# A graph network on one core: drains on POOL at every fourth block of an edge pass

## The reference

```
h = relu(layernorm(x)); x = x + L0(h)   # typed attention: k[src], q[dst], v[src] per edge, softmax over the edges of dst
h = relu(layernorm(x)); x = x + L1(h)   # gated attention: z[src], segment_max, segment_sum, sigmoid gate
h = relu(layernorm(x)); x = x + L2(h)   # U[dst] += w ** [1, 1, 2, 6] * x.sum(1)[src]; U @ coeff.T
h = relu(layernorm(x)); x = x + L3(h)   # three convolutions:
    m = concat(h[dst], h[src], edge_attr) @ W + b
    h = segment_sum(m, dst)             # with relu after the first two
```

## Time and profile before

| | |
|---|---|
| median of 3 timed runs | 11907.75 us |
| lowest and highest | 11903.76 and 11925.74 us |
| span of the profiled execution | 13242.4 us |
| POOL busy in it | 9106.3 us (69%) |
| DVE busy | 4015.6 us (30%) |
| ACT busy | 3476.7 us (26%) |
| PE busy | 1352.0 us (10%) |
| moved by DMA | 919.05 MB, 69 GB/s on average |

### The profile page before, as it was taken

How to read it: one execution, slowest core, us unless ns; L and a number is a source line. 1 busy time by engine, 2 the same in 40 slices (tenths; PEclk the granted TensorE clock), 3 DMA queues, 4 the chain that set the end, 5 groups by cost and what they waited for, 6 DMA issues and landing times. The chain is left out here.

```text
span 13242.4 us, 37433 instructions
## 1 busy us (share of the span) xinstructions
PE 1352.0 (10%) x6735; PEld 1005.3 (8%) x6735; DVE 4015.6 (30%) x5472; ACT 3476.7 (26%) x4561; POOL 9106.3 (69%) x8728
## 2 busy tenths in 40 slices
PE   5200000020000000395000000200000000000000
PEld 3100000010000000273000000200000000000000
DVE  2255555544445544695111111011111101111110
ACT  2333223312222222375232222122211212221121
POOL 3677777767777776402777777577777767777776
PEclk7655555555555555697555555555555555555555
DMA  7333333313333333001222222111111111111111
GB/s 277 133 97 97 98 95 95 100 34 90 98 95 94 94 99 81 14 1 32 61 58 61 58 58 60 40 50 46 49 46 46 49 39 50 46 49 46 46 49 42
DMA packets 404823, 919.05 MB, mean 69 GB/s; under 512 B 171046, under 2 KB 195277, under 8 KB 389496
## 3 DMA queue, kind: packets, MB, share of 16 engines
q0 software_dynamic: 278944, 386.91, 13.3%
q1 hardware_dynamic: 121832, 529.42, 10.9%
q10 hardware_dynamic: 3824, 0.50, 0.0%
HBM read 456.45 MB, written 459.77 MB: 69 GB/s over the span
## 5 line engine op out<-in xcount | busy, mean ns | idle before, releaser
L864 POOL DMA_INDIRECT arena<-tab,src x6256 | 6549.8, 1047 | 2894.4 <-issue 2101.0
L2244 DVE TENSOR_TENSOR_SCAN arena<-cv_keep,arena 128x768 f32<-128x768 f32 (+1 forms) x476 | 752.0, 1627 | 5757.2 <-issue 4526.3
L864 POOL DMA_INDIRECT arena<-tab,spread x1564 | 1644.1, 1051 | 518.5 <-issue 518.5
L2106 ACT COPY arena<-arena 128x1472 f32<-128x1472 f32 x204 | 545.3, 2673 | 3003.9 <-DMA arena<-tab,src 3003.9
L2111 ACT COPY arena<-arena 128x1472 f32<-128x1472 f32 (+1 forms) x204 | 588.3, 2884 | 551.8 <-DVE arena L2244 431.2
L1089 PE MATMUL e_t<-ident,arena 128*68 128x128 f32 (+1 forms) x2 | 0.8, 397 | 4433.5 <-PEq L1433 2223.3
L2168 PE MATMUL cv_t<-ident,arena 128*81 128x128 f32 (+1 forms) x294 | 137.9, 469 | 2917.7 <-ACT arena L2118 1528.3
L2105 ACT COPY arena<-arena 128x368 f32<-128x368 f32 x68 | 55.3, 813 | 1353.7 <-issue 1325.1
L2182 PE MATMUL cv_t<-ident,arena 128*64 128x128 f32 (+1 forms) x3 | 1.3, 425 | 3391.1 <-ACT arena L2111 3391.1
L951 ACT ACTIVATE ae_prob<-arena 128x92 f32<-128x92 f32 x68 | 17.1, 251 | 1228.8 <-remote 1152.7
L1089 PEld LDWEIGHTS e_t<-ident,arena 128*68 128x68 f32 (+1 forms) x2 | 0.3, 134 | 4433.9 <-issue 4433.9
(11 more groups left out here) (370 smaller groups left out, 6943.0 us busy)
## 6 DMA issues: line engine op xcount, KB each, us to landing
rows<-arena SPq DMA_DIRECT2D x68, 1506.5 KB
arena<-tab,src POOLq DMA_INDIRECT x6256
rows3b<-arena SPq DMA_DIRECT2D x136, 736.0 KB
rows<-arena SPq DMA_DIRECT2D x68, 920.0 KB
rows<-arena SPq DMA_DIRECT2D x68, 828.0 KB
tab<-arena SPq DMA_DIRECT2D x49, 1024.0 KB
q_start<-arena SPq DMA_DIRECT2D x32, 1564.0 KB
arena<-q_start SPq DMA_DIRECT2D x68, 736.0 KB
```

Of the source, the lines that this page charges most:

```text
L864: pool.indirect_dma_start(out=rows[b][:, j, :], out_offset=None, in_=table, in_offset=bass.IndirectOffsetOnAxis(ap=idx[:, at:at + 1].bitca ...
L2106: nc.scalar.copy(chain[:, 0:D, 1:C1], rin[b].rearrange("p j f -> p f j")).then_inc(s_in, 1)
L2244: ins = v.tensor_tensor_scan(out=part, data0=keep[:, 0:(f1 - f0) * C1], data1=part, initial=0.0, op0=ALU.mult, op1=ALU.add)
```

## The change

Inside `gather_columns`, behind the wait at the head of a block and ahead of its gathers, POOL now runs a drain where the block's number is a multiple of SWEEP = 4 and not zero. That is at blocks 4, 8, 12 and so on up to 64: 16 drains in a pass, 80 in the program. A drain holds the engine's sequencer until the engine has finished what it was given before. Nothing else is different: the gathers, their order, the waits and the buffers stay, and no instruction of another engine moves.

```diff
@@ -76,6 +76,7 @@
 BATCH = 3
 UNIT = 8
 ARENA = 25600
+SWEEP = 4
 SEG = 32
 SEGS = -(-J // SEG)
 JP = SEGS * SEG
@@ -859,6 +860,8 @@
     for c in range(NC):
         b = c % 2
         wait(pool, s_rows, c - 1)
+        if c and c % SWEEP == 0:
+            pool.drain()
         for j in range(C):
             at = c * C + j
             pool.indirect_dma_start(out=rows[b][:, j, :], out_offset=None, in_=table,
```

## The result

The change makes the kernel slower: 12546.64 us (12543.96 to 12548.2) against 11905.76 us, a ratio of 1.0537 (95% interval 1.0524 to 1.0550). That is 640.9 us, or 8.01 us for each of the 80 drains. The forecast was 0.45 us each.

A forecast was written before the change was run, and what follows sets the result against it. POOL's gathers were taken to bound every pass. Drain plus restart less the usual gap, 0.45 us for each of 80 drains, gave 36 us on the 11907.75 us median: 11944 us, range 11890 to 12100 us.

The forecast's parts named there:

- What bounds the kernel: In the five gather passes POOL sets the pace, one gather every 1.25 us; time added there moves the end equally.
- Is that buffer there in an execution that isn't profiled? The trace speaks against it.: Behind POOL's gathers: a buffer slowing blocks from 28.8 to 32.2 us was taken as absent from timed runs.
- The drain itself: At each new drain: the drain's own time, nearest rows 0.21 us and 0.04 to 0.05 us.
- The restart: From a drain's end to POOL's next gather: 0.28 to 0.92 us, less the usual 0.30 us gap.
- The transfers in flight: Rival at each new drain: it waits for transfers in flight, 1.8 us extra, 141 us in all, 12049 us; chance 0.12.
- The buffer stays full: Rival in the passes: a real, full buffer binds POOL at 1.40 us a gather; 105 us more, 12013 us; chance 0.09.
- emptied cheaply: Rival in the passes: drains empty a real slow buffer cheaply, 192 us less in all, 11716 us; chance 0.10.
- The whole tail is paid and nothing comes back: Rival at each new drain: the full 9.9 us tail is paid, 792 us in all, 12700 us; chance 0.05.
- slow buffer: Behind POOL in the rivals: something paced at 1.40 us per gather that holds POOL when full.
- The chances: For the whole kernel: slower by over 0.2% 0.62, same 0.28, faster 0.10.
- bare cost of drain and restart: Main case at the 80 new drains: 0.45 us each, 11944 us, own range 11905 to 11975; chance 0.64.

The follow-up runs named there:

- second recording: The kernel before, unchanged, profiled once more: span 11903.9 us, against 13242.4 us when it was first profiled.
- Kernel 8: Kernel before with, at the change's 80 places, a wait until the consumer is through with the block, then a drain: 13226.79 us, ratio 1.1110.
- kernels 13 and 14: Kernel before plus 55 drains, at every sixth block: at its head 12160.02 us (ratio 1.0213), 15 gathers later 12111.87 us (1.0172).

## Why the prediction was wrong

The place was right and the size was not: 36 us were forecast for the sum, and 640.9 us measured. Point by point:

- *What bounds the kernel.* Right. POOL's flow of gathers sets the pace of the passes, and the 639.2 us that it gained in gaps came out of the end in full. The changed kernel's groups of four blocks take the 115 us they took before and the 8 us of a hole, and ACT and DVE have no part in it.
- *"Is that buffer there in an execution that isn't profiled? The trace speaks against it."* This is the step that failed. I saw two things, blocks that got slower and long tails of the drains at the ends of stages, and made one cause of them. Since the blocks' slowness couldn't be in the timed runs, I struck out the tails as well. The second recording has the one without the other: all gaps are 0.3 us, and the drain of L908 takes 22.5 us in it against 25.1 us. The 9.9 us tail of the last stage in rows 8 was nearly all real; without the disturbance it is 8.22 us (the drain ends at 11901.83, the last gather at 11893.61).
- *The drain itself.* Mis-sized: 0.04 to 0.21 us were taken from the drains of L1063 and L198. They were thought quick because POOL had been quiet. Kernel 8 shows that quiet doesn't help. The drains of L1063 and L198 follow no more than two DMAs since the last drain, and 0.21 us for two and 0.05 us for none fit 0.0817 us a DMA. The row to be read was the drain of L1619, behind 197 DMAs, which is shown below; the sum had at most 0.21 us.
- *The restart.* Within its bounds: 0.72 us from the drain's end to the next gather, against 0.28 to 0.92 us.
- *The transfers in flight* (first rival, 12049 us). Its mechanism is there as a floor of some 1.6 us that shows behind short runs; behind 92 gathers it is covered by the clearing. Of the two passages of the Trainium skill weighed beside the sum, Perfetto Trace Analysis ("DMA Instruction — SWDGE (GPSIMD)") says that a gather's row ends when its last descriptor is written; the trace agrees, with ACT starting 1.45 us behind that end. PSUM — Partial Sum Buffer ("Engine vs sequencer instructions") says that a drain waits until its engine is fully idle. From the two the prediction took it that nothing beyond the rows is waited for. The runs show 7.57 us beyond them behind 92 gathers.
- *The buffer stays full, or is emptied cheaply* (12013 and 11716 us). There is no such buffer holding POOL back in a timed run.
- *The whole tail is paid and nothing comes back* (12700 us, chance 0.05). This is what happened in size, with 7.57 us of tail for the 9.9 us of the disturbed recording and 0.42 us of restart beyond the usual gap; but what stands behind the tail is not the slow buffer of the rivals. The argument against it, that the trace has tail and stalls only together, was wrong on the first recording itself. The stage of L1619 runs undisturbed there (its gathers and scatters come with gaps of 0.30 us as in the second recording), and its last DMA is this:

```profile
5489.67 1.05 POOL L1649 DMA_INDIRECT arena<-s_tab,first  x1 [0.30 <-issue]
```

The drain of L1619 begins at 5473.1 us and lasts 25.8 us, so it ends 8.14 us after this DMA. That is a tail without a stall, and the second recording has the same 8.14 us.

- *The chances.* 0.62 for slower was on the right side, though most of it rested on the bare cost of drain and restart, which is not what was paid. The range, up to 12100 us, left out the one case whose price stood in a row of the trace.

Shown by the runs: the 0.0817 us a gather up to 112, that idling of up to 15.8 us doesn't reduce it, that in a pass at one pace a clearing without a drain sets in at 113 to 115 open gathers, and what it takes there (kernels 13 and 14). Only argued: that the 0.0817 us are the sequencer's bookkeeping of each transfer, and that in plain flow it is hidden because the sequencer is some twelve gathers (15 us) ahead. Open: what disturbed the first recording, whether the count or the time sets off a clearing, how far it goes outside the passes, and the longer holes of the first two passes.

No version beats the kernel before. Its own long drains at the ends of stages could not be shortened by met waits.

## What to carry to other kernels

A drain on POOL in the middle of a run of indirect DMAs is priced by the gathers since the last drain, here 0.08 us each up to about 112 and at least some 1.6 us right behind a gather, plus 0.7 us of restart. Idle time ahead of it doesn't lower the 0.08 us each; where only landing matters, a wait on the semaphore is cheaper (2.28 against 8.01 us here). Read a new drain's cost from the existing drain that has most like it in front. And where the profiled span and the timed runs differ by 11%, record again before a term is taken out of the sum on the ground of that difference.

## What the runs showed of the hardware

- A drain of POOL takes 0.0817 us for each indirect DMA that POOL has issued since the last drain (tails of 3.16 us behind 38 and 9.20 us behind 112), after they have landed. Some holes of the first two passes are up to 3.7 us longer. An idle time of 4.2 to 15.8 us ahead of the drain takes nothing off (7.55 to 7.64 us behind 92 or 93 DMAs, all 80 times).
- In a pass, at 113 to 115 open gathers, POOL clears on its own, up to the last head of a block (46 of 138 left with a head at 92, 38 of 138 with one at 100), with no gap in the gathers. At the end of the convolutions 100 are left (8.22 us), which that rule doesn't give.
- POOL's sequencer runs about twelve gathers ahead: a drain's row starts that much before the last gather and reads 22.5 us where the hole is 8.29 us.
